# Normalisation statistics three groups ahead instead of two in the routing stage of a mixture-of-experts block

## The chip, the cores and the metric

The kernel runs on one core of a Trainium2 chip. The metric is device time in microseconds (us) of one execution; lower is better. The core's engines are TensorE (PE; its weight loads are shown as PEld), VectorE (DVE), ScalarE (ACT), GpSimd (POOL) and SyncE (SP), which here issues only transfers. Each engine works its own list of instructions in order, and waits on semaphores that others raise.

## The reference

`x` has 2 x 4096 tokens of 256 numbers. Three parts follow each other: half a mixture-of-experts feed-forward block, a delta-rule attention block, and the same feed-forward block again.

```
x = x + 0.5 * ffn(layernorm(x), gate_w, w1, w2, w3)
x = x + attn(layernorm(x), ...)
x = x + 0.5 * ffn(layernorm(x), gate_w, w1, w2, w3)

def ffn(x, gate_w, w1, w2, w3):            # 8 experts, the best 2 of each token
    scores = softmax(x @ gate_w)
    top_scores, top_idx = top_k(scores, 2)
    xs = scale.T[:, :, None] * x            # scale: top_scores at top_idx, else 0
    h = silu(xs @ w1) * (xs @ w3)           # for each expert
    return (h @ w2).sum(over experts)
```

## The kernel before

The change is in the function `ffn`, in what it does only for the first feed-forward block (`first_stage`). That block has a routing stage and an expert stage.

**The routing stage** takes the 8192 tokens in eight groups (m = 0 to 7, `NG` = 8) of 8 x 128 tokens (`GB` = 8). One group is 1 MB of `x` in one of four buffers `xb[:, m % 4]`. For each group:

- SP loads it (`load_x`, L354). Groups 0 to 3 go out at the start. Group m from 4 on goes into the buffer of group m - 4, so SP first waits until all eight scatters of group m - 4 have landed.
- DVE takes mean and variance (`ln_stats`, L539 and L542: eight BN statistics and eight aggregates), after waiting for the load.
- POOL turns the variance into a reciprocal deviation (`inverse_std`, L811 and L813).
- PE transposes the tokens (`turn_tokens`, L414), ACT copies them out (`turned`, L733), and PE multiplies them with the gate weights (`logits`, L425).
- DVE corrects the products by mean and deviation (`norm_products`, L559 to L568), picks two experts (`choose`, L574 to L604), and makes scores (`scores`) and extra columns of the row (`row_ends`).
- PE counts places within the lists of the experts (`positions`, L441 to L446), and DVE makes row numbers of them (`places`, L630 to L642).
- POOL writes the group's rows into the list of their best expert in device memory: `scatter(m)`, eight indirect transfers (L819) which read the row numbers of `places(m)`.

The order on each engine is written out by hand. DVE first does the statistics of groups 0 and 1 and clears some buffers. Then it waits for the column sums of the gate weights from PE (`column_sums_out`, L547). For each m it then does `norm_products`, `choose`, `scores`, `row_ends`, `places`, `ln_stats(m + 2)` and, from m = 1, `split_low(m - 1)`, a part of the expert weights (L646). POOL does `inverse_std(0)` and `inverse_std(1)` among its constants, then for each m `scatter(m)` and `inverse_std(m + 2)`. PE does for each m `turn_tokens(m + 1)`, `positions(m)`, `logits(m + 1)`.

After the last group DVE works out a table of tiles (`work_out`, L145 to L176), and SP fills up the ends of the lists from it (`fill_ends`, L187).

**The expert stage** starts when all rows of all lists have landed: SP and ACT wait for all scatters (`wait_scattered`, L342), and SP then loads the first rows from the lists (L366). Everything after it, the attention block and the second feed-forward block, follows in sequence.

Of the kernel before, what the change touches and what calls it, by code (L numbers as in the profile page):

```python
# [17 lines left out]
NG = NT // GB  # L18
# [21 lines left out]
def wait(eng, sem, value):  # L40

    if not (isinstance(value, int) and value <= 0):
        eng.wait_ge(sem, value)
# [166 lines left out]
def ffn(nc, name, src, rows1, rows2, sums, kept, fresh, first_stage):  # L210
# [13 lines left out]
    with ctx:  # L224
# [119 lines left out]
        def table_row(k, which, engine, most):  # L344
            _, got = nc.values_load_multi_w_load_instructions(
                tab[0:1, which, TPB * k:TPB * (k + 1)], engines=[engine], min_val=0, max_val=most,
                skip_runtime_bounds_check_because="the table holds sums of at most seven ones, and rows of the lists")
            return got
# [184 lines left out]
        def _(dve):  # L533
            def ln_stats(m):
                dve.wait_ge(x_loaded[m % 4], 16 * (m // 4 + 1))
                wait(dve, stats_ready, m)
                wait(dve, row_made, 3 * (m - 3))
                for j in range(GB):
                    dve.bn_stats(stats[:, j, :], xb[:, m % 4, j, 0:DM]).then_inc(stats_part, 1)  # L539
                dve.wait_ge(stats_part, GB * (m + 1))  # L540
                for j in range(GB):
                    last = dve.bn_aggr(mv[:, m % 4, j, :], stats[:, j, :])  # L542
                last.then_inc(stats_ready, 1)

            def column_sums_out():
                dve.wait_ge(colsum_done, 1)
                dve.tensor_copy(colsum[:], pos[:, 0:E]).then_inc(colsum_ready, 1)  # L547
# [6 lines left out]
            def norm_products(m):  # L554

                n = NORM * m
                dve.wait_ge(rstd_ready, m + 1)
                dve.wait_ge(colsum_ready, 1)
                dve.tensor_tensor(shift[:], mv[:, m % 4, :, 0], rstd[:, m % 4], ALU.mult).then_inc(norm_part, 1)  # L559
                dve.wait_ge(lg_done, 2 * (m + 1))  # L560
                dve.tensor_tensor(scaled_lg[:], lg[:, 0:GB * E].rearrange("p (j e) -> p j e", e=E), over(rstd[:, m % 4]),
                                  ALU.mult).then_inc(lg_read, 1)
                dve.wait_ge(norm_part, (NORM - 1) * m + 1)
                dve.tensor_tensor(shift_lg[:], over(shift[:]), colsum[:].unsqueeze(1).broadcast_to([P, GB, E]),
                                  ALU.mult).then_inc(norm_part, 1)
                dve.wait_ge(norm_part, (NORM - 1) * m + 2)
                dve.wait_ge(lg_read, m + 1)
                dve.tensor_tensor(normed_lg[:], scaled_lg[:], shift_lg[:], ALU.subtract).then_inc(norm_part, 1)  # L568
# [38 lines left out]
            def scores(m):  # L607
                dve.wait_ge(exp_ready, m + 1)
                dve.tensor_reduce(lsum[:], lexp[:, :, 0:E], AX.X, ALU.add).then_inc(scl_part, 1)
                dve.wait_ge(scl_part, 2 * m + 1)  # L610
                dve.reciprocal(scl[:, 0], lsum[:]).then_inc(scl_part, 1)
                dve.wait_ge(scl_part, 2 * m + 2)
                dve.tensor_tensor(scl[:, 1], lexp[:, :, E], scl[:, 0], ALU.mult).then_inc(scl_ready, 1)
# [30 lines left out]
            def split_low(e):  # L644
                dve.wait_ge(w_hi, e + 1)
                dve.tensor_tensor(ws[:, e, 1], stage[:, e], ws[:, e, 0].bitcast(F32), ALU.subtract).then_inc(w_lo, 1)  # L646
# [38 lines left out]
                    dve.tensor_tensor(lo, raw, hi.bitcast(F32), ALU.subtract).then_inc(attn_lo, 1)  # L685

            if first_stage:
                for m in range(2):
                    ln_stats(m)
                for buf in (picked, upto2, upto4, upto8):  # L690
                    dve.memset(buf[:, :, 0:GB], 0.0).then_inc(cleared, 1)
                table.zeros(dve, cleared)
                dve.wait_ge(cleared, 8)
                dve.wait_ge(consts, CONSTS)
                column_sums_out()
                for m in range(NG):
                    norm_products(m)
                    choose(m)
                    scores(m)
                    row_ends(m)  # L700
                    places(m)
                    if m + 2 < NG:
                        ln_stats(m + 2)
                    if m == NG - 1:
                        dve.wait_ge(row_part, ROWS * NG)
                        table.work_out(dve, nextrow[:, NG % 2], tab, past, skipped, tab_step, tab_ready)
                    if m > 0:
                        split_low(m - 1)
                split_low(NG - 1)
# [95 lines left out]
        @block.gpsimd  # L805
        def _(pool):
            def inverse_std(m):
                pool.wait_ge(stats_ready, m + 1)
                wait(pool, rstd_ready, m)
                wait(pool, row_made, 3 * (m - 3))  # L810
                pool.tensor_scalar(var_eps[:], mv[:, m % 4, :, 1], EPS, None, ALU.add).then_inc(rstd_part, 1)  # L811
                pool.wait_ge(rstd_part, m + 2)
                pool.tensor_tensor(rstd[:, m % 4], var_eps[:], mhalf[:], ALU.pow).then_inc(rstd_ready, 1)  # L813

            def scatter(m):
                pool.wait_ge(row_part, ROWS * (m + 1))
                pool.wait_ge(row_made, 3 * (m + 1))
                for j in range(GB):
                    pool.indirect_dma_start(  # L819
                        out=rows1, out_offset=bass.IndirectOffsetOnAxis(ap=slots[:, m % 2, j:j + 1], axis=0),  # L820
                        in_=xb[:, m % 4, j, :], in_offset=None).then_inc(scattered[m % 4], 16)

            def put(k):
                pool.wait_ge(to_ready, k + 1)
                for j in range(TPB):
                    if j % 2 == 0:
                        pool.wait_ge(y_ready, 2 * k + j // 2 + 1)
                    pool.indirect_dma_start(  # L828
                        out=rows2 if k < NSP else sums,
                        out_offset=bass.IndirectOffsetOnAxis(ap=to[:, k % NW, j:j + 1], axis=0),  # L830
                        in_=xw[k % NW][:, j] if k < NSP else xw[k % NW][:, j, 0:DM], in_offset=None,
                        bounds_check=(NROWS if k < NSP else B * L) - 1, oob_is_err=False).then_inc(stored[k % NW], 16)

            if first_stage:
                pool.memset(mhalf[:], -0.5).then_inc(rstd_part, 1)
                pool.memset(ident[:], 0.0).then_inc(id_set, 1)
                pool.wait_ge(id_set, 1)
                pool.affine_select(out=ident[:], in_=ident[:], compare_op=ALU.not_equal, fill=1.0, base=0,
                                   pattern=[[-1, P]], channel_multiplier=1).then_inc(id_set, 1)
                inverse_std(0)  # L840
                pool.memset(before[:], 1.0).then_inc(consts, 1)
                pool.wait_ge(consts, 1)
                pool.affine_select(out=before[:], in_=before[:], compare_op=ALU.is_ge, fill=0.0, base=-1,
                                   pattern=[[1, P]], channel_multiplier=-1).then_inc(consts, 1)
                pool.memset(ones[:], 1.0).then_inc(consts, 1)
                inverse_std(1)
                pool.iota(rank[:], [[-1, E]], base=E, channel_multiplier=0, allow_small_or_imprecise_dtypes=True)\
                    .then_inc(consts, 1)
                pool.iota(nextrow[:, 0], [[0, 2], [REGION, E]], base=0, channel_multiplier=0,
                          allow_small_or_imprecise_dtypes=True).then_inc(consts, 1)  # L850
                pool.iota(goal[:], [[P, NT]], base=0, channel_multiplier=1,
                          allow_small_or_imprecise_dtypes=True).then_inc(consts, 1)
                table.constants(pool, consts)
            if first_stage:
                for m in range(NG):
                    scatter(m)
                    if m + 2 < NG:
                        inverse_std(m + 2)
            for k in range(NST):
                put(k)  # L860

# [1464 lines left out]
```

## Time and profile before

| | |
|---|---|
| Runs (device time) | 1526.34, 1530.04 and 1530.6 us, median 1530.04 |
| The profiled execution | 1526.34 us, of it 1524.6 us span |
| Routing stage, first scatter to last | 25.27 to 120.53 us of the span |
| First loads of the expert stage | 122.69 us |
| Whole span, busy | PE 84%, DVE 71%, ACT 63%, POOL 63% |

The shares in the last line are means over stages with different limits. The change touches only the first 125 us, so the stage has to be read by itself, engine by engine in order of time. A timeline row gives the start, the duration, the engine, the line, the operation with what it writes and reads, and, in brackets, how long the engine had been idle before it and what released it.

### The profile page before, as it was taken

What the parts mean: (1) busy time and instruction counts of PE and PEld (TensorE: products, weight loads), DVE (VectorE), ACT (ScalarE), POOL (GpSimd) and SP (SyncE); (2) the same over time, 40 slices, a digit from 0 to 9 for tenths busy, and PEclk for the clock granted to TensorE, in tenths of its full rate; (3) what the DMA queues carried; (4) which work ended last, traced back from release to release, by engine and by line L of the source; (5) the groups of instructions that cost most, each with busy time, mean ns of one, the idle gap of its engine ahead of it and who ended that gap; (6) DMA issues with size and microseconds to landing.
All of it is one profiled execution on the core that took longest, in us unless ns stands there. A gap on an engine that the chain in (4) does not pass through costs nothing. (4 is left out here: it accounts for less than half of the span.)

```text
span 1524.6 us, 38923 instructions
## 1 busy us (share of the span) xinstructions
PE 1286.8 (84%) x12840; PEld 1179.8 (77%) x12840; DVE 1084.7 (71%) x2722; ACT 954.5 (63%) x1948; POOL 965.5 (63%) x1716
## 2 busy tenths in 40 slices
PE   7965994996579999999999999999998724994996
PEld 7864993995468888888888888888887623993996
DVE  6873772674668889888888898888986462672674
ACT  2214772772377777878788787787876424772773
POOL 4872673566366757677677877776877441774566
PEclk8556996998699999999999999999999856997998
DMA  7547976681012212222322222223222265776682
GB/s 222 170 137 204 306 248 222 229 278 68 23 27 48 51 45 51 76 60 68 80 60 72 74 63 79 61 63 86 61 78 59 73 192 182 255 258 218 239 274 83
DMA packets 224034, 196.04 MB, mean 129 GB/s; under 512 B 105556, under 2 KB 186714, under 8 KB 223840
## 3 DMA queue, kind: packets, MB, share of 16 engines
q1 hardware_dynamic: 190560, 117.21, 27.6%
q0 software_dynamic: 24576, 67.94, 12.1%
q10 hardware_dynamic: 8704, 8.39, 1.8%
q8 instruction: 111, 1.82, 0.5%
q14 instruction: 83, 0.68, 0.2%
HBM read 103.68 MB, written 96.10 MB: 131 GB/s over the span
## 5 line engine op out<-in xcount | busy, mean ns | idle before, releaser
L1550 DVE SCALAR_TENSOR_TENSOR raw_w<-attn_raw,taps,raw_w 128x256 f32<-128x256 f32 x576 | 246.0, 489 | 28.5 <-ACT raw_w L1932 28.4
L468 PE MATMUL ffn_both<-ws,ffn_xhi 128*128 x1152 | 203.8, 289 | 0.5
L457 PE MATMUL ffn_both<-ident,ffn_xb 128*128 128x128 f32 x576 | 82.0, 290 | 101.3 <-ACT ffn_xb L753 101.3
L468 PEld LDWEIGHTS ffn_both<-ws,ffn_xhi 128*128 128x128 f32 x1152 | 164.1, 192 | 3.1 <-issue 3.1
L2217 POOL TENSOR_TENSOR attn_inv<-attn_inv,attn_term 64x14 f32<-64x14 f32 (+6 forms) x448 | 132.3, 295 | 35.1
L457 PEld LDWEIGHTS ffn_both<-ident,ffn_xb 128*128 128x128 f32 x576 | 70.1, 150 | 103.5 <-ACT ffn_xb L753 81.9
L2214 POOL TENSOR_TENSOR attn_term<-attn_small,attn_inv 64x14 f32<-64x14 f32 (+6 forms) x448 | 125.2, 279 | 32.6
L1202 PE MATMUL attn_fr<-attn_xhi,wqkv 128*128 128x256 f32 x768 | 138.8, 290 | 4.0 <-ACT attn_bth L1939 2.4
L491 PE MATMUL ffn_yb<-ws,ffn_hhi 128*128 x576 | 119.3, 291 | 6.2 <-DVE ffn_hlo L667 6.2
L1202 PEld LDWEIGHTS attn_fr<-attn_xhi,wqkv 128*128 128x128 f32 x768 | 109.3, 193 | 15.6 <-issue 10.6
L828 POOL DMA_INDIRECT second_rows<-ffn_more_rows,ffn_to x64 | 63.1, 985 | 84.6 <-DVE ffn_to L652 68.6
L468 PE MATMUL ffn_both<-ws,ffn_xlo 128*128 x576 | 116.0, 283 | 0.0
L662 DVE TENSOR_TENSOR ffn_hid<-ffn_both,ffn_sil 128x512 f32<-128x512 f32 x72 | 49.8, 691 | 90.3 <-ACT ffn_sil L765 90.3
L657 DVE TENSOR_TENSOR ffn_xlo<-ffn_both,ffn_xhi 128x1024 fp32r<-128x1024 f32 x72 | 87.7, 1218 | 36.6 <-ACT ffn_xhi L760 36.3
L753 ACT ACTIVATE ffn_xb<-ffn_more_rows 128x256 f32<-128x256 f32 x120 | 62.1, 591 | 81.8 <-DMA ffn_more_rows<-first_rows 47.2
L765 ACT ACTIVATE ffn_sil<-ffn_both 128x512 f32<-128x512 f32 x72 | 43.0, 597 | 92.4 <-PE ffn_both L468 92.4
L491 PEld LDWEIGHTS ffn_yb<-ws,ffn_hhi 128*128 128x128 f32 x576 | 94.1, 191 | 7.2 <-issue 7.2
L760 ACT ACTIVATE ffn_xhi<-ffn_both 128x1024 fp32r<-128x1024 f32 x72 | 73.9, 1026 | 33.8 <-PE ffn_both L457 33.8
L2157 POOL DMA_INDIRECT first_rows<-attn_xg,attn_slots x64 | 70.3, 1098 | 34.6 <-issue 16.5
L468 PEld LDWEIGHTS ffn_both<-ws,ffn_xlo 128*128 128x128 f32 x576 | 90.0, 191 | 0.0
L1932 ACT ACTIVATE raw_w<-attn_raw,taps 128x256 f32<-128x256 f32 x192 | 86.9, 500 | 2.0
L1262 PE MATMUL attn_tp<-ws 64*128 64x256 f32 x512 | 75.4, 415 | 11.6 <-DVE ws L1584 8.9
(310 smaller groups left out, 3879.4 us busy)
## 6 DMA issues: line engine op xcount, KB each, us to landing
ffn_more_rows<-second_rows SPq DMA_DIRECT2D x56, 259.0 KB
ffn_xb<-second_rows SPq DMA_DIRECT2D x48, 259.0 KB, 4.9
raw_w<-second_rows SPq DMA_DIRECT2D x40, 259.0 KB
ffn_more_rows<-first_rows SPq DMA_DIRECT2D x64, 131.0 KB
ffn_xb<-in_L_attn_x_dram SPq DMA_DIRECT2D x8, 1024.0 KB, 5.8
attn_xin<-x_after_first ACTq DMA_DIRECT2D x32, 256.0 KB, 2.8
attn_xres<-x_after_first SPq DMA_DIRECT2D x32, 256.0 KB, 3.0
x_after_attention<-attn_xres SPq DMA_DIRECT2D x32, 256.0 KB, 2.2
```

The costliest lines, as they stand in the source:

```text
L457: last = pe.transpose(tr[:, q, j * P:(j + 1) * P], xs[:, k % 2, j, q * P:(q + 1) * P], ident[:])
L468: last = pe.matmul(hp[:, j, :], (xhi, xlo)[b][:, k % 2, q, j * P:(j + 1) * P], ws[:, bass.ds(experts[j], 1), a, q].rearrange("p o d -> p ( ...
L491: last = pe.matmul(yb[:, j, :], (hhi, hlo)[b][:, k % 2, j * P:(j + 1) * P], ws[:, bass.ds(experts[j], 1), a, 2].rearrange("p o d -> p (o d)"),
L657: dve.tensor_tensor(xlo[:, k % 2], tr, xhi[:, k % 2].bitcast(F32), ALU.subtract).then_inc(xlo_ready, 1)
L760: act.activation(xhi[:, k % 2], tr, ACT.Copy).then_inc(xhi_ready, 1)
L1202: last = pe.matmul(out, w[:, a, q, col], (xhi, xlo)[b][:, q, :], skip_group_check=True, start=(start and k == 0 and q == 0), stop=(k == 2 ...
L1262: last = pe.matmul(tp[:, h, s * 2 * P:(s + 1) * 2 * P], kq[a, par, q, s, 0, :], kq[a, par, q, s], start=(s == 0), stop=True, skip_group_ch ...
L1550: dve.scalar_tensor_tensor(acc[:, j, r], raw[:, j, r, :, tap:tap + P], taps[:, j, r, tap:tap + 1], acc[:, j, r], ALU.mult, ALU.add)\
L1932: act.activation(acc[:, j, r], raw[:, j, r, :, 0:P], ACT.Copy, scale=taps[:, j, r, 0:1])\
L2157: pool.indirect_dma_start(out=rows1, out_offset=bass.IndirectOffsetOnAxis(ap=slots[:, j:j + 1], axis=0), in_=xg[:, j, :], in_offset=None). ...
L2214: pool.tensor_tensor(term[:, 0:k, 0:j], n[:, j + 1:, j:j + 1].broadcast_to([BP, k, j]), v[:, j:j + 1, 0:j].broadcast_to([BP, k, j]), ALU.m ...
L2217: pool.tensor_tensor(v[:, j + 1:, 0:j], v[:, j + 1:, 0:j], term[:, 0:k, 0:j], ALU.subtract)\
```

## The change

The statistics of a group are taken three groups ahead instead of two. DVE does `ln_stats` of groups 0, 1 and 2 before the loop, and `ln_stats(m + 3)` after `places(m)`. POOL does `inverse_std(2)` between the fourth and the fifth transfer of `scatter(0)`, and `inverse_std(m + 3)` after `scatter(m)`. No other instruction is added or taken away, the buffers stay as they are (four of `xb`, of `mv` and of `rstd`), and PE, ACT and SP keep their order.

```diff
@@ DVE
             if first_stage:
-                for m in range(2):
+                for m in range(3):
                     ln_stats(m)
...
                     places(m)
-                    if m + 2 < NG:
-                        ln_stats(m + 2)
+                    if m + 3 < NG:
+                        ln_stats(m + 3)
@@ POOL, in scatter(m), after the indirect transfer j
+                    if m == 0 and j == 3:
+                        inverse_std(2)
...
                 for m in range(NG):
                     scatter(m)
-                    if m + 2 < NG:
-                        inverse_std(m + 2)
+                    if m + 3 < NG:
+                        inverse_std(m + 3)
```

## Rows read from the trace of the kernel before

**Rows 1.** Busy time by engine in the stretch of the scatters (count of instructions in brackets)

```profile
core 0: us, PE busy (x) PEld busy (x) DVE busy (x) ACT busy (x) POOL busy (x), PEclk, DMA share, GB/s
25.30:120.60 95.30, 70.60 (x348) 68.42 (x348) 75.16 (x330) 19.42 (x27) 76.05 (x76) 0.55 0.44 146
```

**Rows 2.** Timeline of POOL: first and last transfers of scatters

```profile
25.27 1.22 POOL L819 DMA_INDIRECT first_rows<-ffn_xb,ffn_slots  x1 [8.53 <-DVE ffn_xb L642]
...
34.43 0.96 POOL L819 DMA_INDIRECT first_rows<-ffn_xb,ffn_slots  x1 [0.30 <-issue]
...
37.63 1.10 POOL L819 DMA_INDIRECT first_rows<-ffn_xb,ffn_slots  x1 [0.19 <-issue]
...
47.43 0.96 POOL L819 DMA_INDIRECT first_rows<-ffn_xb,ffn_slots  x1 [0.30 <-issue]
...
50.62 1.10 POOL L819 DMA_INDIRECT first_rows<-ffn_xb,ffn_slots  x1 [0.20 <-issue]
...
59.61 0.96 POOL L819 DMA_INDIRECT first_rows<-ffn_xb,ffn_slots  x1 [0.30 <-issue]
...
62.80 1.09 POOL L819 DMA_INDIRECT first_rows<-ffn_xb,ffn_slots  x1 [0.19 <-issue]
...
110.22 0.96 POOL L819 DMA_INDIRECT first_rows<-ffn_xb,ffn_slots  x1 [0.30 <-issue]
...
119.57 0.96 POOL L819 DMA_INDIRECT first_rows<-ffn_xb,ffn_slots  x1 [0.30 <-issue]
```

**Rows 3.** Timeline of DVE in the routing stage

```profile
12.46 0.64 DVE L542 BATCH_NORM_AGGREGATE ffn_mv<-ffn_stats 128x2 f32<-128x6 f32 x8
...
17.95 0.17 DVE L547 COPY ffn_colsum<-ffn_pos 128x8 f32<-128x8 f32 x1 [4.19 <-PE ffn_pos L433]
...
24.86 2.70 DVE L539 BATCH_NORM_STATS2 ffn_stats<-ffn_xb 128x6 f32<-128x256 f32 x8
...
35.75 2.70 DVE L539 BATCH_NORM_STATS2 ffn_stats<-ffn_xb 128x6 f32<-128x256 f32 x8
...
39.89 0.16 DVE L559 TENSOR_TENSOR ffn_shift<-ffn_mv,ffn_rstd 128x8 f32<-128x8 f32 x1
...
46.58 0.29 DVE L630 TENSOR_TENSOR ffn_row<-ffn_pos,ffn_nextrow 128x128 f32<-128x128 f32 x1 [0.69 <-PE ffn_pos L446]
...
53.39 0.22 DVE L561 TENSOR_TENSOR ffn_scaled_lg<-ffn_lg,ffn_rstd 128x64 f32<-128x64 f32 x1 [1.31 <-PE ffn_lg L425]
...
59.39 0.29 DVE L630 TENSOR_TENSOR ffn_row<-ffn_pos,ffn_nextrow 128x128 f32<-128x128 f32 x1 [0.68 <-PE ffn_pos L446]
...
60.59 2.70 DVE L539 BATCH_NORM_STATS2 ffn_stats<-ffn_xb 128x6 f32<-128x256 f32 x8
...
99.81 0.17 DVE L559 TENSOR_TENSOR ffn_shift<-ffn_mv,ffn_rstd 128x8 f32<-128x8 f32 x1 [3.00 <-POOL ffn_rstd L813]
...
108.61 0.17 DVE L642 COPY ffn_xb<-ffn_slot 128x8 f32<-128x8 f32 x1
...
115.99 0.31 DVE L176 TENSOR_TENSOR tab<-rows,last_row 128x144 int32<-128x144 f32 x1
```

**Rows 4.** Timeline of SP's queue: loads of groups 2, 4, 5, first expert loads

```profile
2.44 1.72 SPq L354 DMA_DIRECT2D ffn_xb<-in_L_attn_x_dram  x1
...
37.14 0.37 SPq L354 DMA_DIRECT2D ffn_xb<-in_L_attn_x_dram  x1
...
51.09 0.37 SPq L354 DMA_DIRECT2D ffn_xb<-in_L_attn_x_dram  x1
...
122.69 7.24 SPq L366 DMA_DIRECT2D ffn_more_rows<-first_rows  x12
```

**Rows 5.** Transfers: issue to landing of groups 4 and 5, then of all eight

```profile
ffn_xb<-in_L_attn_x_dram SPq DMA_DIRECT2D x1, 1024.0 KB, 5.6
...
ffn_xb<-in_L_attn_x_dram SPq DMA_DIRECT2D x1, 1024.0 KB, 6.0
...
DMA to landing us min/median/max: 5.3/5.8/11.1
```

**Rows 6.** Waits of POOL, 25 to 125 us: total, times, longest

```profile
POOL first_rows L819 <- DVE ffn_xb L642: 8.5, 1, 8.5
```

## The prediction

> **What bounds the kernel now.** The chain of work that ended last does not reach back into the first 125 us, so I read the stage of the change by itself, in this order. The busy times by stretch come first: between 25.3 and 120.6 us POOL and DVE are both busy for about 76 of 95 us, so the shares alone don't name a bound [rows 1]. POOL's timeline does. After its first scatter, which DVE releases at 25.27 us, each transfer follows the one before at a steady step: seven steps from 50.62 to 59.61 are 8.99 us, 1.28 each, and the next scatter starts at 62.80 [rows 2]. POOL's waits of this stretch hold just one for DVE, the 8.5 us before the first scatter [rows 6]; the rest is a gap of 0.2 to 0.3 us before each transfer, which belongs to its issue. So POOL sets the pace, at 12.18 us a group (50.62 to 62.80) as long as one `inverse_std` goes with it. That leaves 3.20 us from the last transfer of group 0 to the first of group 1 (34.43 to 37.63) where a plain step is 1.28, so an `inverse_std` costs 1.92 us [rows 2]. POOL's last transfer starts at 119.57, the first loads of the expert stage at 122.69, 3.12 us later [rows 2, 4].
>
> DVE keeps up: it waits now and then, 3.00 us for POOL's reciprocal deviation before group 7 and 1.31 us for PE's logits before group 3 [rows 3], and none of it reaches POOL. A wait of DVE for a load of `x` does not occur inside the loop. The loads explain it. Group 4 goes out at 37.14, 2.71 us after the last transfer of group 0 started, and takes 5.6 us; group 5 goes out at 51.09, 3.66 us after that of group 1, and takes 6.0 [rows 2, 4, 5]. Group 4 lands at 42.7, and DVE wants it only after the places of group 2.
>
> **The change, part by part.**
>
> *Statistics of group 2 before the loop.* They cost DVE about 3.3 us, as the other groups' (eight of 2.70 in sum and the aggregates' 0.64) [rows 3]. They start at 13.1, when those of group 1 end, if the data is there: its load started at 2.44 and the slowest of all eight took 11.1, so it is there by 13.5 at the latest [rows 3 to 5]. They end by 16.9, the memsets that now fill 13.1 to 13.8 end by 17.6, and the wait for the column sums, now 4.19 us long, ends at 17.95 [rows 3]. Cost nothing, hidden by that wait; without it, 3.3 us. The first scatter stays at 25.27.
>
> *`inverse_std(2)` inside scatter(0).* POOL does six of them after 25.3 us either way, so its sum is unchanged. But the last transfer of group 0 starts 1.92 us later, at 36.35, the load of group 4 at 39.06, and its landing at 44.66. Scatter(1) starts at 37.63 + 1.92 = 39.55.
>
> *Statistics three ahead.* This is the step that counts. `ln_stats(m + 3)` stands right behind `places(m)` and needs the load of group m + 3, which needs the buffer of group m - 1, whose scatter POOL began only a group ago. Before, the statistics of group m + 2 needed scatter m - 2. One of the four buffers' worth of slack is gone. Behind the waiting instruction are queued `split_low`, `norm_products`, `choose` and `places` of the next group on DVE, behind these `positions` and the next `logits` on PE, and the next scatter on POOL.
>
> The durations: from the start of statistics to the next `norm_products` 4.14 us (35.75 to 39.89), 0.16 more to its second instruction (L561). From that to the end of `places` 7.20 (53.39 to 60.59). From L630 to the end of `places` 1.20 (59.39 to 60.59). From L630 to the next L561, where PE's logits bind, 6.81 (46.58 to 53.39). From the end of `places` to the scatter 0.41 (24.86 to 25.27) [rows 2, 3]. From a scatter's start to its last transfer 8.99, then 2.71 to the load and 5.6 to its landing [rows 2, 4, 5].
>
> - DVE ends places(1) at 35.75 as now, and waits for group 4 until 44.66, 8.9 us. L561 of group 2 at 44.66 + 4.30 = 48.96, places(2) end 56.16, scatter(2) at 56.57. POOL was free at 39.55 + 12.18 = 51.73: 4.8 us idle.
> - Group 5 lands at 39.55 + 8.99 + 8.31 = 56.85. L561 of group 3 at 61.15 by that, at 54.96 + 6.81 = 61.77 by the logits. Places(3) end 68.97, scatter(3) at 69.38 (POOL free at 68.75).
> - Group 6 lands at 56.57 + 17.30 = 73.87, which holds DVE for 4.9 us. Places(4) end at 73.87 + 4.30 + 7.20 = 85.37, scatter(4) at 85.78 (POOL free at 81.56).
> - Group 7 lands at 69.38 + 17.30 = 86.68. L561 of group 5 at 90.98, by the logits the same. Places(5) end 98.18, scatter(5) at 98.59 (POOL free at 97.96).
> - No statistics are left. Groups 6 and 7 go at the pace of logits and places, 6.81 + 7.20 - 1.20 = 12.81 each: places(7) end at 123.80, scatter(7) at 124.21.
>
> Scatter(7) starts at 110.22 now [rows 2]: 14.0 us later. The loop in it is scatter, landing, load, statistics, choice, scatter: 17.30 + 11.50 + 0.41 = 29.2 us for two groups, where POOL alone needs 24.4.
>
> What is late next: the table ends 7.4 us after `places(7)` (108.61 to 115.99) [rows 3], so at 131.2. The last transfer starts 9.35 us after scatter(7) does (110.22 to 119.57), at 133.6, and the expert loads 3.12 later at 136.7 instead of 122.69. All that follows waits for them and is unchanged. Sum: +14.0 us.
>
> *Bounds.* With the slower scatter(1) seen now (9.80, 37.63 to 47.43) and the slower load (3.66 + 6.0 = 9.66) [rows 2, 4, 5] for groups 5 and 7, places(5) end at 101.9 and the sum is +17.7. Below, the pace of the last two groups is open. It depends on PE's clock: the granted clock was 0.55 over the stretch, mostly the lower level of 1.2 GHz [rows 1], and one period was only 10.89 us (24.86 to 35.75) [rows 3]. With two such periods scatter(7) starts at 120.4, +10.1; if only POOL bound them (8 x 1.28 = 10.3 each), at 119.1, +8.9. I take the slow pace, since the new waits leave PE less busy than now.
>
> The load of 1 MB took 5.6 and 6.0 us [rows 5]. The Trainium skill (DMA: Bandwidth & Descriptors, Anatomy of one DMA) fits a transfer that GpSimd issues as 2.0 us plus its bytes at 436 GB/s, which is an estimate of 4.4 us here. The trace does not agree, for loads that SP issues beside scatters. By that figure the same walk gives +11.6.
>
> **The rivals.**
>
> - *Paced by the logits or POOL at the end* (described as the lower bound): +9 to +10 us. For it: periods of 10.9 occur. Against: the clock of the stretch [rows 1].
> - *Loads slower still*, because each now starts where the next scatter does and both write or read device memory: above +17.7, about +20 with 2 us more on either of the two loads in the decisive path. For it: one of the two loads shown left 0.95 us later than the other and took 0.4 more. Against: POOL's new idle time leaves fewer scatters beside them.
> - *No change*: POOL stays the bound and hides DVE's new wait. For it: POOL has no other wait [rows 6] and the amount of its work is the same. This decides at one point: scatter(2) must be released by 51.73, which needs group 4 landed by 51.73 - 0.41 - 7.20 - 4.30 = 39.8, but its load only leaves at 39.06 and the fastest took 5.3 [rows 5]. Price 0, the time stays at about 1529. The Trainium skill (Perfetto Trace Analysis, Identifying the Most-Contended Engine) says to work first on the engine with the highest occupancy, by which a move of DVE's work beside a saturated POOL would be worth nothing; here the order of DVE decides when POOL is fed.
> - *Faster*: the earlier deviation spares DVE its 3.00 us before group 7 [rows 3]. It could help only if POOL then had less to do, and it hasn't: 0 to -3 us at most.
>
> **How the numbers follow.** The profiled execution took 1526.34 us with a span of 1524.6. The sum gives 1540.3 for it. It was the fastest of three runs with a mean of 1529.0 and a median of 1530.04, so I put the time at 1529.0 + 14.0 = 1543. Chances: forecast (+11 to +17.7) 0.74, paced by logits or POOL 0.12, slower loads 0.06, no change 0.06, faster 0.02. Range: from the lower bound on the fastest run, 1526.3 + 8.9 = 1535, taken down to 1534, to 1530.6 + 17.7 = 1548.3, taken up to 1549. Within 0.3% (4.6 us) is what a measurement of this kernel can't tell from no change. Three of the cases are slower by more: 0.92. Same 0.06, faster 0.02.
>
> **What would show it.** Right: DVE's waits hold L539 for the loads of `x` near 36 us (about 9 us) and near 69 us (about 5); POOL idles before scatters 2, 4, 6 and 7, on DVE L642, for some 5, 4, 2 and 3 us; scatter(1) starts near 39.6, the expert loads near 136.7; from there on the stages last as long as before. Wrong at the first step: the column sums later than 17.95, scatter(0) later than 25.3. Wrong as a whole: group 4 landed by 40, or POOL without gaps.

## The result, and the profile after

The changed kernel took 1544.03 us in the median of five runs (1538.71 to 1548.08), where the kernel before took 1530.6 (1526.34 to 1536.58). The ratio is 1.008, with a 95% interval of 1.0056 to 1.0103, so between 8.6 and 15.8 us slower, the middle near 12; the two medians are 13.4 us apart. The forecast was 1543 us, +14.0. The profiled execution has a span of 1540.5 us where before it was 1524.6.

First POOL's waits of the stretch from 0 to 140 us in the changed kernel: total, times, longest.

```profile
POOL first_rows L819 <- DVE ffn_xb L642: 18.1, 3, 8.9
POOL first_rows L819 <- issue: 17.6, 59, 0.3
```

Before there was one wait for DVE, the 8.5 us ahead of the first scatter [rows 6]. Now there are three, and two of them, 9.2 us together, are new. POOL's timeline says where they are, and that POOL does not stop again after them.

```profile
25.75 1.22 POOL L819 DMA_INDIRECT first_rows<-ffn_xb,ffn_slots  x1 [8.94 <-DVE ffn_xb L642]
...
33.07 1.10 POOL L819 DMA_INDIRECT first_rows<-ffn_xb,ffn_slots  x1 [0.20 <-POOL ffn_rstd L813]
...
40.20 1.10 POOL L819 DMA_INDIRECT first_rows<-ffn_xb,ffn_slots  x1 [0.20 <-issue]
...
56.77 1.09 POOL L819 DMA_INDIRECT first_rows<-ffn_xb,ffn_slots  x1 [4.58 <-DVE ffn_xb L642]
...
69.56 1.10 POOL L819 DMA_INDIRECT first_rows<-ffn_xb,ffn_slots  x1 [0.20 <-issue]
...
86.64 1.10 POOL L819 DMA_INDIRECT first_rows<-ffn_xb,ffn_slots  x1 [4.60 <-DVE ffn_xb L642]
...
99.68 1.09 POOL L819 DMA_INDIRECT first_rows<-ffn_xb,ffn_slots  x1 [0.20 <-issue]
...
120.78 0.96 POOL L819 DMA_INDIRECT first_rows<-ffn_xb,ffn_slots  x1 [0.30 <-issue]
```

These are the first transfers of scatters 0, then (33.07) the fifth transfer of scatter(0) behind the reciprocal deviation, then scatters 1, 2, 3, 4, 5 and 7. Scatter(7) starts at 120.78 where it was 110.22 [rows 2].

Why POOL waited for the places of groups 2 and 4 stands in DVE's timeline.

```profile
18.03 0.17 DVE L547 COPY ffn_colsum<-ffn_pos 128x8 f32<-128x8 f32 x1 [0.70 <-PE ffn_pos L433]
18.71 0.17 DVE L559 TENSOR_TENSOR ffn_shift<-ffn_mv,ffn_rstd 128x8 f32<-128x8 f32 x1 [0.52 <-DVE ffn_colsum L547]
...
37.21 0.17 DVE L642 COPY ffn_xb<-ffn_slot 128x8 f32<-128x8 f32 x1
44.98 2.71 DVE L539 BATCH_NORM_STATS2 ffn_stats<-ffn_xb 128x6 f32<-128x256 f32 x8 [7.61 <-DMA ffn_xb<-in_L_attn_x_dram]
...
57.22 2.71 DVE L539 BATCH_NORM_STATS2 ffn_stats<-ffn_xb 128x6 f32<-128x256 f32 x8 [0.74 <-DMA ffn_xb<-in_L_attn_x_dram]
...
74.85 2.71 DVE L539 BATCH_NORM_STATS2 ffn_stats<-ffn_xb 128x6 f32<-128x256 f32 x8 [6.21 <-DMA ffn_xb<-in_L_attn_x_dram]
...
87.16 2.71 DVE L539 BATCH_NORM_STATS2 ffn_stats<-ffn_xb 128x6 f32<-128x256 f32 x8 [0.81 <-DMA ffn_xb<-in_L_attn_x_dram]
...
98.38 0.17 DVE L642 COPY ffn_xb<-ffn_slot 128x8 f32<-128x8 f32 x1
...
108.52 0.17 DVE L642 COPY ffn_xb<-ffn_slot 128x8 f32<-128x8 f32 x1
...
119.18 0.17 DVE L642 COPY ffn_xb<-ffn_slot 128x8 f32<-128x8 f32 x1
```

Each of the four statistics in the loop that need a reused buffer now waits for its load, two for long (7.61 and 6.21 us) and two for short (0.74 and 0.81). SP's queue has the rest: the load of group 4 leaves at 39.46 instead of 37.14, and the first loads of the expert stage at 133.60 instead of 122.69 [rows 4].

```profile
39.46 0.37 SPq L354 DMA_DIRECT2D ffn_xb<-in_L_attn_x_dram  x1
...
133.60 7.24 SPq L366 DMA_DIRECT2D ffn_more_rows<-first_rows  x12
```

So 10.9 of the 15.9 us between the two profiled executions come from the routing stage. The other 5.0 came later, and the first experiment asks whether they belong to the change.

### The profile page after: what moved, and what is told of

The parts are those of the page before. It is cut to its first block and busy times, and to the rows that moved or that the text cites. A ratio compares the mean times of both kernels' runs of the same rounds, so it can differ in the third digit from the quotient of the medians.

```text
span 1540.5 us, 38923 instructions
## 1 busy us (share of the span) xinstructions
PE 1281.9 (83%) x12840; PEld 1176.3 (76%) x12840; DVE 1083.6 (70%) x2722; ACT 954.4 (62%) x1948; POOL 965.6 (63%) x1716
## 5 line engine op out<-in xcount | busy, mean ns | idle before, releaser
L819 POOL DMA_INDIRECT first_rows<-ffn_xb,ffn_slots x64 | 65.5, 1023 | 36.3 <-DVE ffn_xb L642 18.1
```

## The experiments

Each ratio is to the kernel before, run on the same chip beside it (24 runs with a median of 1528.3 us on one chip, 29 with 1528.64 us on the other).

### Both kernels once more

No edit. How much of the later difference is chance, and does TensorE's clock change the pace of the last groups?

> The kernel before, unchanged, profiled and timed once more. The first expert loads again within 0.5 us of 122.7 us, POOL without a gap from its first scatter to its last. It also shows how much the later stages move between two executions of one program: if the 5.0 us by which the changed kernel's execution grew beyond the 10.9 us of the routing stage (15.9 in all) are chance, then two executions of this one program differ by some 3 to 5 us after 122.7 us as well; if they belong to the change, this one repeats 1402 us from the first expert load to the end within 1 us. Time ratio 1.000.

> The changed kernel, unchanged, once more. First expert loads at 133.6 us if TensorE's clock rises again before the last two groups (periods of 10.3 and 10.7 us from places to places), at up to 137 if it stays at its lower level (12.8 us each, the pace that the prediction took). POOL again idles some 4.6 us before scatters 2 and 4. From the first expert load to the end 1402 us plus what chance adds. Ratio 1.008.

The kernel before: ratio 0.9995 (0.998 to 1.001), first expert loads at 121.69 us, span 1521.4. So the loads went out 1.0 us earlier than in its first execution, where 0.5 was expected at most. The changed kernel: ratio 1.0077 (1.0048 to 1.0106), span 1540.3, first expert loads at 136.03 us, so 2.4 us later than in its first execution. POOL's timeline of this execution shows the difference: its waits before scatters 0, 2 and 4 are there again, and two more before scatters 6 and 7.

```profile
56.39 1.10 POOL L819 DMA_INDIRECT first_rows<-ffn_xb,ffn_slots  x1 [4.33 <-DVE ffn_xb L642]
...
85.48 1.09 POOL L819 DMA_INDIRECT first_rows<-ffn_xb,ffn_slots  x1 [4.33 <-DVE ffn_xb L642]
...
111.16 1.41 POOL L819 DMA_INDIRECT first_rows<-ffn_xb,ffn_slots  x1 [2.50 <-DVE ffn_xb L642]
...
123.95 0.95 POOL L819 DMA_INDIRECT first_rows<-ffn_xb,ffn_slots  x1 [2.52 <-DVE ffn_xb L642]
```

DVE's timeline of the same execution gives the cause, a wait for PE's logits. The same wait was 2.45 us long in the first execution (at 112.07), and before group 6 it was 2.54 against 4.58:

```profile
110.71 0.17 DVE L642 COPY ffn_xb<-ffn_slot 128x8 f32<-128x8 f32 x1
...
116.39 0.23 DVE L561 TENSOR_TENSOR ffn_scaled_lg<-ffn_lg,ffn_rstd 128x64 f32<-128x64 f32 x1 [4.58 <-PE ffn_lg L425]
...
123.50 0.17 DVE L642 COPY ffn_xb<-ffn_slot 128x8 f32<-128x8 f32 x1
```

The last two periods, from places to places, were 12.89 and 12.79 us here, and 10.14 and 10.66 in the first execution. The busy times of the two stretches, first of the first execution and then of this one, show the granted clock in the third number from the end:

```profile
99.00:119.00 20.00, 13.47 (x76) 12.87 (x76) 12.92 (x60) 3.92 (x6) 15.54 (x16) 0.59 0.26 94
```

```profile
98.00:124.00 26.00, 18.71 (x86) 18.11 (x86) 14.02 (x65) 3.93 (x6) 16.52 (x18) 0.50 0.23 83
```

At 0.50 the clock stood at its lower level, 1.2 GHz, throughout; at 0.59 it was at 2.4 GHz for part of the stretch. PE's timeline shows what that does to the 32 matmuls of the logits of group 7, first of the first execution and then of this one:

```profile
107.20 4.83 PE L425 MATMUL ffn_lg<-ffn_gws,ffn_xT 128*128 128x8 f32 x32
```

```profile
109.38 6.97 PE L425 MATMUL ffn_lg<-ffn_gws,ffn_xT 128*128 128x8 f32 x32
```

One program, two paces.

From the first expert load to the end of the span the kernel before took 1401.9 and 1399.7 us in its two executions, the changed one 1406.9 and 1404.3. The expectation allowed either reading here: the two executions of the kernel before differ by 2.2 us, less than the 3 it named for chance and more than the 1 it named for the change. The other kernels below, whose program behind the routing stage is that of the kernel before, except for a fifth buffer in two, took 1402.4 to 1406.4. The 1406.4 belong to a kernel with ratio 1.0005, so most of the 5.0 us is within what executions differ by anyway. The 1406.9 lie 0.5 us above the highest of the others; a share of the change in them is neither shown nor excluded.

### A fifth buffer of x

```diff
-        xb = sb("xb", [P, 4, GB, ROW])
+        xb = sb("xb", [P, 5, GB, ROW])
...
-                wait(sp, scattered[m % 4], 16 * GB * (m // 4))
-                sp.dma_start(xb[:, m % 4, :, 0:DM], x_v[m]).then_inc(x_loaded[m % 4], 16)
+                wait(sp, scattered[m % 5], 16 * GB * (m // 5))
+                sp.dma_start(xb[:, m % 5, :, 0:DM], x_v[m]).then_inc(x_loaded[m % 5], 16)
```

All other uses of `xb`, `x_loaded` and `scattered` follow. Once in the changed kernel, once in the kernel before:

> The changed kernel with five buffers of x in place of four, so that the load of group m + 3 waits for the scatter of group m - 2 and not of m - 1. Theory (DVE's wait for the load is the whole loss): DVE waits for no load in the loop, POOL runs without a gap again, scatter(7) starts at 110.2 to 111, the first expert loads go out at 122.7 to 123.5, and the time is that of the kernel before within 0.2%. Rival (the reciprocal deviation inside scatter(0), or the new place of the statistics beside POOL's transfers, costs by itself): first expert loads stay near 133 us, ratio 1.008.

> The kernel before with five buffers of x, statistics two ahead as before. It tells whether the 2.7 us by which the changed kernel with five buffers was still behind (125.4 against 122.7) belong to the buffers or to the order. Theory (order and TensorE's clock: first scatter late, and groups at 12.8 us by the logits): first expert loads at 121.7 to 122.7 us as in the two executions of the kernel before. Rival (the fifth buffer costs, by an earlier load of group 4 beside the expert weights): 124 us or later.

The changed kernel with five buffers: ratio 1.0012 (0.9995 to 1.0028), so from 0.8 us faster to 4.3 us slower than the kernel before. The loss of 12 us is gone. DVE's waits from 20 to 140 us hold no load of `x` any more:

```profile
DVE ffn_scaled_lg L561 <- PE ffn_lg L425: 14.9, 7, 4.5
DVE ffn_xlo L657 <- ACT ffn_xhi L760: 8.9, 2, 5.2
DVE ffn_to L652 <- DMA ffn_more_rows<-first_rows: 7.2, 1, 7.2
DVE ffn_row L630 <- PE ffn_pos L446: 4.1, 6, 0.7
```

The first expert loads went out at 125.39 us, later than the 122.7 to 123.5 expected, and POOL did stop once more, 2.17 us before scatter(7) at 113.12, for the places. The kernel before with five buffers has ratio 1.002 (1.0003 to 1.0038) and 124.11 us, which just meets its rival's "124 us or later". So the rest of the gap is not seen to be the order's: with five buffers the two orders give the same time within their intervals. In the first of them DVE waited for the logits in every group (seven waits, 14.9 us), with periods of 11.9 to 12.9 us from places to places. Whether the fifth buffer itself costs a microsecond or two stays open.

### POOL in its old order

```diff
-                    if m == 0 and j == 3:
-                        inverse_std(2)
...
-                    if m + 3 < NG:
-                        inverse_std(m + 3)
+                    if m + 2 < NG:
+                        inverse_std(m + 2)
```

> DVE takes the statistics three ahead, POOL keeps its old order (reciprocal deviation two ahead, none inside scatter(0)). Theory: the loss stays, since DVE's wait stays. The load of group 4 leaves 1.9 us earlier than in the changed kernel, at about 37.5, DVE's wait ends at about 43.1, scatters 1 to 5 start 1.9 to 2.1 us earlier, but one more reciprocal deviation stands among the last three scatters, so that scatter(7) starts at about 120 and the first expert loads go out at about 133. Rival (what POOL does inside scatter(0) is the loss): first expert loads near 123 us.

Ratio 1.0056 (1.0036 to 1.0075). The load of group 4 left at 37.11 us and DVE's wait for it ended at 42.41; scatters 1 to 5 started 2.3 to 3.5 us earlier than in the changed kernel. Scatter(7) started at 118.91, the first expert loads at 131.56, of 133 expected. The last two groups ran in 10.20 and 10.77 us from places to places, so this execution compares with the first one of the changed kernel. Most of the loss stays with DVE's order alone. POOL's old order gives back 2 of 11 us in these two profiled executions, as far as it lets the loads go earlier; the intervals of the two ratios overlap, so the times do not show that gain.

### Group 2 ahead, and nothing else

```diff
-                for m in range(2):
+                for m in range(3):
                     ln_stats(m)
...
-                    if m + 2 < NG:
+                    if 0 < m and m + 2 < NG:
                         ln_stats(m + 2)
```

POOL does the same: in the first kernel `inverse_std(2)` stands inside scatter(0) as in the change, in the second before scatter(0), where POOL is idle.

> Only the first part of the change: the statistics of group 2 before the loop and its reciprocal deviation inside scatter(0); all other groups stay two ahead. Theory: DVE waits for no load, POOL runs without a gap. The first scatter starts some 0.5 us late, as in all kernels with these statistics before the loop (25.6 to 26.2 against 25.2), first expert loads at 122 to 123.2 us, ratio 1.000. Rival (the reciprocal deviation inside scatter(0) costs 1.9 us or more): first expert loads at 124.5 us or later.

> As group2_alone, but POOL takes the reciprocal deviation of group 2 before scatter(0), in the 8 us in which it waits there anyway. POOL then has five of them between its scatters instead of six, 1.9 us less. Theory (POOL's sequence sets the end): first scatter 0.5 us late, scatter(1) as soon as places(1) are made, at 36 to 37.5, first expert loads 0.5 to 1.5 us before those of the kernel before, at 121 to 122 us. Rival (DVE's and PE's loop, 12.8 us a group at TensorE's lower clock, is the bound as soon as POOL has less to do): no gain, 122.5 us or later. Both ratios within 0.999 to 1.001.

The first: ratio 1.0006 (0.9985 to 1.0028), first expert loads at 123.85 us, between theory and rival. Scatter(0) began at 25.66, 0.4 to 0.5 us late, and scatter(1) at 38.14 where it was 37.63 [rows 2] and 37.46, so hardly more than that lateness: the reciprocal deviation inside scatter(0) costs 0.2 us at most by itself. The second: ratio 1.0005 (0.9989 to 1.0021), first expert loads at 125.60. Here the rival holds. POOL had 1.9 us less to do, and idled instead:

```profile
39.52 0.95 POOL L819 DMA_INDIRECT first_rows<-ffn_xb,ffn_slots  x1 [2.62 <-DVE ffn_xb L642]
52.33 1.10 POOL L819 DMA_INDIRECT first_rows<-ffn_xb,ffn_slots  x1 [0.91 <-DVE ffn_xb L642]
113.22 0.96 POOL L819 DMA_INDIRECT first_rows<-ffn_xb,ffn_slots  x1 [0.42 <-DVE ffn_xb L642]
```

DVE waited seven times for the logits there, 13.0 us in all, where it was 9.2 us in the kernel with the deviation inside scatter(0). Scatter(0) itself started at 26.75, 1.5 us late and not the 0.5 expected, but that does not hide a gain: from there to the first expert loads it took 98.9 us, against 98.2 in the other kernel and 97.4 and 96.5 in the two executions of the kernel before. POOL's 12.2 us a group and the 12.8 us of PE and DVE at the lower clock lie too close for a saving on POOL alone. No kernel of this study beats the one before.

### Four ahead

DVE takes the statistics of groups 0 to 3 before the loop and `ln_stats(m + 4)` after `places(m)`; the rest is the changed kernel.

```diff
-                for m in range(3):
+                for m in range(4):
                     ln_stats(m)
...
-                    if m + 3 < NG:
-                        ln_stats(m + 3)
+                    if m + 4 < NG:
+                        ln_stats(m + 4)
```

> The suspected wait made longer: DVE takes the statistics four groups ahead, POOL keeps the order of the changed kernel. The statistics of group m + 4 then need the scatter of the very group whose places were just made, so every loop of scatter, landing, load, statistics and choice holds one group and not two: 0.4 + 9.0 + 2.6 + 5.5 + 4.3 + 7.2 = 29 us for each of the scatters 1 to 4. Theory: POOL starts scatter(4) near 146 us, scatter(7) at 177 to 184, the first expert loads go out at 189 to 197 us, the time grows by 67 to 74 us over the kernel before (ratio 1.044 to 1.049). Rival (the loss comes from the new order of POOL, which is the same as in the changed kernel): ratio 1.008.

Ratio 1.0452 (1.0415 to 1.0488), median 1596.81 us of two runs, first expert loads at 193.23. POOL's timeline shows the loop with one group in it:

```profile
58.50 1.10 POOL L819 DMA_INDIRECT first_rows<-ffn_xb,ffn_slots  x1 [15.56 <-DVE ffn_xb L642]
...
87.07 1.09 POOL L819 DMA_INDIRECT first_rows<-ffn_xb,ffn_slots  x1 [16.58 <-DVE ffn_xb L642]
...
115.75 1.10 POOL L819 DMA_INDIRECT first_rows<-ffn_xb,ffn_slots  x1 [16.70 <-DVE ffn_xb L642]
...
144.35 1.54 POOL L819 DMA_INDIRECT first_rows<-ffn_xb,ffn_slots  x1 [16.60 <-DVE ffn_xb L642]
```

Scatters 1, 2, 3 and 4 are 28.57, 28.68 and 28.60 us apart, where the loop's terms add up to 29. The rival, that POOL's order is the loss, is far off.

| kernel | ratio | first expert loads, us |
|---|---|---|
| before (two executions) | 1; 0.9995 | 122.69; 121.69 |
| changed (two executions) | 1.008; 1.0077 | 133.60; 136.03 |
| changed, five buffers | 1.0012 | 125.39 |
| before, five buffers | 1.002 | 124.11 |
| changed, POOL in its old order | 1.0056 | 131.56 |
| group 2 ahead alone | 1.0006 | 123.85 |
| the same, on POOL before scatter(0) | 1.0005 | 125.60 |
| four ahead | 1.0452 | 193.23 |

## Why the prediction was right, point by point

**Statistics of group 2 before the loop** were put at nothing, hidden by the wait for the column sums. Nearly so: that wait shrank from 4.19 us [rows 3] to 0.70 and the copy behind it came at 18.03 instead of 17.95. But the next instruction then came 0.52 us after the copy had ended, and the first scatter at 25.75 instead of 25.27. Some 0.5 us that the sum lacks. The same 0.52 us stand in all six executions that take three groups' statistics ahead of the loop, and not in the one that takes four. A late first scatter alone does not prove it: with five buffers and the old order it started at 25.91, because DVE waited 0.69 us for PE's positions.

**The reciprocal deviation inside scatter(0)**: the load of group 4 at 39.06 by forecast, 39.46 measured, which is the 0.5 us again. By itself it costs 0.2 us at most, as the kernel with group 2 alone shows.

**The wait for the loads** is the cause, as forecast. The load of group 4 was expected at 44.66 and let the statistics go at 44.98. The long waits were forecast at 8.9 and 4.9 us and are 7.6 and 6.2: DVE reached the first 1.6 us later than in the walk (most of it 0.5 from the late start, and 11.94 us for group 1 where the walk kept the 10.89 of the kernel before), and the load behind the second landed 1.0 us later. POOL's idle time before scatters 2 and 4 was forecast at 4.8 and 4.2, and is 4.58 and 4.60. Three runs tie the loss to this wait. A buffer that takes the wait away takes the loss away (1.0012); a wait with one group less in its loop makes it more than five times as large (1.0452); DVE's order alone keeps most of it (1.0056). The loop of two groups was forecast at 29.2 us; scatters 2 to 4 and 3 to 5 are 29.87 and 30.12 apart. At the end of places(5), forecast at 98.18, the two executions stood at 98.55 and 97.99, so up to there the walk is right in size as well.

The loads of 1 MB took 5.4 to 5.6 us in the changed kernel, not the 4.4 of the estimate from the Trainium skill (DMA: Bandwidth & Descriptors, Anatomy of one DMA). They were not slower than before either, so the rival of slower loads is out. The durations of the trace are the ones to add up, which makes the sum 14.0 and not 11.6; the timing (8.6 to 15.8) can't tell the two.

**The pace of the last two groups** is the term that was set too fixed. The prediction took 12.81 us for each, the pace of the logits at the lower clock, and named the faster one as a rival at 0.12. The first profiled execution ran them in 10.14 and 10.66 us, and POOL did not wait for them: scatter(7) at 120.78, within 2 us of the 119.1 of that rival. The second ran them in 12.89 and 12.79, and scatter(7) started at 123.95, where the forecast has 124.21. One program shows both, so this was no either-or to be given a chance, but a spread of 3 us between executions; how often each pace occurs is not known. The reason given for the slow one, that the new waits leave PE less busy, is not borne out. From 79 to 97 us PE was busy for 12.4 us in the first execution and for 13.6 in the second, at granted clocks of 0.53 and 0.50; from 97 to 109 the less busy one was granted 0.72 and the other 0.50. That the measured ratios, 1.008 and 1.0077, stand for 12 us and not 14.0 is what a mix of the two would give, though the intervals are too wide to show it.

**What is late next**: the table was ready in time, and the first expert loads followed the last transfer as before. The stages behind show nothing beyond what executions of one program differ by.

**No change**, given 0.06, failed at the point it was tied to: group 4 had to land by 39.8 and landed at 45.0. Its argument, work beside a saturated POOL is free, is right only while the other engine keeps POOL fed. The rival *faster* gained nothing, though DVE's wait for the deviation before group 7 was gone as it said.

## What to carry to other kernels

Looking further ahead on one engine is not free when the data comes through a ring of buffers. With n buffers, a stage that reads d groups ahead waits for the release of group m + d - n; take the whole loop (last use, landing, reload, work up to the next last use) and divide it by the groups in it, and compare that with the period of the bound. Here it was 29 us for two groups, 14.6 us each, against 12.2 us a group on POOL. With one buffer more the loop holds three groups, by the same sum (an estimate) under 10 us each, and the loss was gone. And before saving work on the engine that has no gaps, look at how close the next one is: 1.9 us less on POOL gained nothing.

## What the runs showed that was not expected

- The pace of the routing stage differs between executions of one program by TensorE's clock: the same pair of groups took 20.8 and 25.7 us with granted clocks of 0.59 and 0.50 over that stretch.
- With the wait for the column sums cut from 4.2 to 0.7 us, DVE's next instruction starts 0.52 us after the copy instead of 0.10. With four groups ahead the copy comes at 20.83 without a wait, and the next instruction 0.10 us after it. No wait that the profile shows explains it; why stays open.
- The granted clock of a page can mislead. In the changed kernel with five buffers it reads 1.00 up to 60 us, yet each of the 109 logits matmuls recorded from 14 to 60 us took 361 ns, as they do where the clock reads 0.50; in the first execution of the changed kernel most of those from 97.5 to 113 us took 256 ns. The duration of the matmuls is the surer sign.
